# Attention memory of a fused layer: tokens grouped as 4p + j, the decayed sums in 16 narrow matmuls, neighbour pairs on GpSimd

## The reference

```python
write_lines = exterior(w1, w2)          # (B, T, 16, 6), from x of the token before and x
read_lines = exterior(r1, r2)           # (B, T, 16, 6)
outer = Jw[..., :, None] * Jw[..., None, :]            # 6 x 6 for each token and head
M = exclusive cumsum over tokens of outer * decay**-pos, times decay**pos
rd_M = einsum('bhti,bhtij->bhtj', rd, M)
mem_score = (1 - alpha) * sum(rd_M * rd) + alpha * sum(rd_M * rd_M)
gated = mean over heads of sigmoid(mem_score * mem_scale) * gate
out = (softmax attention + gated * mem_val) @ out_w.T + out_b
```

## Time and profile before

| | us |
|---|---|
| median of 3 executions | 1076.8 (1074.87 to 1082.2) |
| the profiled execution, its own time | 1076.55 |
| its span | 1074.9 |
| PE busy | 948.6 (88%) |
| DVE busy | 738.0 (69%) |
| ACT busy | 603.7 (56%) |
| POOL busy | 444.0 (41%) |
| mean granted clock of PE, share of full speed | 0.949 |

### The profile page before, as it was taken

The page is one execution under the profiler, slowest core; times in us unless marked ns, Lnnn a source line. Parts: engine busy times, 40 slices in busy tenths (PEclk is TensorE's granted clock), DMA queues, the critical chain, the costliest instruction groups (busy, mean ns, idle before and its releaser), DMA issues. The chain is left out here.

```text
span 1074.9 us, 26814 instructions
## 1 busy us (share of the span) xinstructions
PE 948.6 (88%) x8038; PEld 686.6 (64%) x8039; DVE 738.0 (69%) x2668; ACT 603.7 (56%) x1358; POOL 444.0 (41%) x398
## 2 busy tenths in 40 slices
PE   3698999897998997989979889999989989999970
PEld 1244656554655564565545668888879869889860
DVE  4637797795896996978868668876555655555663
ACT  3155554562563554545535668776676656666653
POOL 6437064273363543654544633322322433222243
PEclk8689999998999999999999999999999989999995
DMA  4785103213124033032030453232333323323264
GB/s 140 247 216 141 31 22 124 56 57 117 38 71 119 24 95 85 2 125 55 21 129 12 139 188 85 45 51 48 49 46 60 73 49 53 48 49 49 41 204 159
DMA packets 60852, 90.38 MB, mean 84 GB/s; under 512 B 8700, under 2 KB 50192, under 8 KB 59696
## 3 DMA queue, kind: packets, MB, share of 16 engines
q1 hardware_dynamic: 45336, 62.20, 20.4%
q0 software_dynamic: 14112, 22.42, 11.2%
q10 hardware_dynamic: 1280, 4.19, 1.0%
HBM read 52.79 MB, written 35.86 MB: 82 GB/s over the span
## 5 line engine op out<-in xcount | busy, mean ns | idle before, releaser
L1926 DVE CUSTOM_DVE_ANT_0 junk<-sm,mask_ts 128x512 bf16<-128x512 f32 (+3 forms) x512 | 220.4, 487 | 58.0 <-PE sm L1366 55.8
L1110 ACT ACTIVATE arena_b<-st 128x512 f32<-128x512 f32 x320 | 180.9, 599 | 136.7 <-PE st L1328 89.8
L950 POOL DMA_INDIRECT sums<-arena_b x66 | 109.9, 1666 | 273.9 <-DVE arena_b L2135 263.6
L2098 DVE TENSOR_TENSOR arena_b<-arena_b 128x256 f16<-128x256 f32 x280 | 116.4, 427 | 109.6 <-ACT arena_b L1185 99.4
L1326 PE MATMUL st<-arena_a 128*128 128x384 f16 (+3 forms) x512 | 129.4, 309 | 29.0 <-issue 19.0
L1366 PE MATMUL sm<-arena_a 128*128 128x512 f16 (+3 forms) x512 | 113.7, 311 | 12.1 <-DVE maxes L1926 6.2
L1518 PE MATMUL st<-arena_b,arena_a 128*128 128x256 f16 x840 | 116.2, 276 | 1.6 <-ACT arena_b L1185 1.6
L1518 PE MATMUL sm<-arena_b,arena_a 128*128 128x256 f16 x840 | 115.1, 273 | 2.3 <-issue 2.3
L1531 PE MATMUL pv<-arena_a,arena_b 128*128 x864 | 116.7, 273 | 0.0
L1531 PE MATMUL sm<-arena_a,arena_b 128*128 x816 | 112.9, 274 | 3.1 <-issue 3.1
L1326 PEld LDWEIGHTS st<-arena_a 128*128 128x128 f16 x512 | 50.9, 99 | 87.0 <-issue 45.2
(11 more groups left out here) (335 smaller groups left out, 1756.5 us busy)
## 6 DMA issues: line engine op xcount, KB each, us to landing
arena_b<-slots SPq DMA_DIRECT2D x35, 260.0 KB
arena_a<-w SPq DMA_DIRECT2D x8, 1024.0 KB, 6.2
arena_b<-x_tr SPq DMA_DIRECT2D x8, 512.0 KB, 4.1
q_rows<-arena_b SPq DMA_DIRECT2D x32, 128.0 KB
k_rows<-arena_b SPq DMA_DIRECT2D x32, 128.0 KB
arena_a<-q_rows SPq DMA_DIRECT2D x32, 128.0 KB
arena_a<-k_rows SPq DMA_DIRECT2D x32, 128.0 KB
res<-x_tok POOLq DMA_DIRECT2D x8, 512.0 KB, 6.4
```

The lines of the kernel that those rows point to most:

```text
L950: pool.indirect_dma_start(sums, bass.IndirectOffsetOnAxis(ap=token_now[:, 1 - par, m:m + 1], axis=0), y_out[1 - par][:, m, :], None, compu ...
L1110: act.activation(probs[:, q, :], st_ps[piece % 2][:, :], ACT.Exp, scale=SCORE_SCALE).then_inc(exp_done, 1)
L1926: last = dve.tensor_tensor_reduce(junk[:, n % 3, at:at + width], sm_ps[n % 3][:, at:at + width], mask_ts[:, T - width:T], 1.0, NEG, ALU.ad ...
L2098: dve.tensor_tensor(g_lo[par][:, hc, :], g_32[:, hc % 4, :], g_hi[par][:, hc, :], ALU.subtract).then_inc(hid_done, 1)
```

## The change

**Token order.** Outside attention proper, partition p now holds the four tokens 4p + j, j = 0 to 3. The loads and stores of the residual, the token numbers, and the weights that PE loads for `values_in` (second half), `lines_in` and `o_tokens` follow it: they are taken with a step of four elements. `values_in` becomes two matmuls of 256 columns in place of one of 512, since its first half stays in the old order.

**Memory.** GpSimd sums the four scaled outer products of a partition (L943 of the changed kernel) in place of building the two extra blocks; PE has one matmul of 36 columns for each head, in two stages of eight heads. What the four tokens of one partition give to each other, six pairs, is worked out on GpSimd (L914 to L922, and L948 to L959) and added by DVE in `memory_scores`. GpSimd has 28 linked instructions in place of 16, with the first pair work ahead of its wait for the norms and the rest behind the signal `outer_done`. DVE multiplies each of the two banks with four read lines in turn (L2015) and reduces 1152 elements at once.

**Start.** The decay table halves, and GpSimd builds two small tables (`tables_of_powers`: powers of the decay for the six pairs) ahead of step 1. **Order.** The stage table is rewritten: two `memory` stages stand where six stood, `z` 0 and some others move.

```diff
+("gates", 0), ("logits", 0), ("values", 6), ("scores", 29), ("maxima", 14), ("memory", 0), ("maxima", 15), ("scores", 30),
+("scores", 31), ("maxima", 16), ("tables", 0), ("scores", 32), ("values", 7), ("rank", 0), ("first_weights", 3),
+("first_expert", 0), ("maxima", 17), ("maxima", 18), ("scores", 33), ("maxima", 19), ("values", 8), ("memory", 1),
+("scores", 34), ("maxima_rows", 0), ("scores", 35), ("scores", 36), ("scores", 37), ("first_rows", 0), ("scores", 38),
...
-sp.dma_start(sums[bass.ds(value(b * T), T), :].rearrange("(c p) d -> p c d", p=P), res_of[par][:, :, 0:D]).then_inc(x1_out_s, 16)
+sp.dma_start(sums[bass.ds(value(b * T), T), :].rearrange("(p c) d -> p c d", c=C), res_of[par][:, :, 0:D]).then_inc(x1_out_s, 16)
...
+    write, read = (lines[:, k, :, :].rearrange("p (c h) e -> p c h e", c=C) for k in range(2))
+    for own in range(C - 1):
+        m, at = C - 1 - own, FIRST_PAIR[own]
+        seen = chain(pool.tensor_tensor(pair_parts[:, at:at + m], read[:, own + 1:C, :, ::-1],
+                                        write[:, own:own + 1].broadcast_to([P, m, H, NL]), ALU.mult))
+    pool.wait_ge(pool_chain, n_of(seen))
+    seen = chain(pool.tensor_tensor(pair_parts[:, :, :, 0:3], pair_parts[:, :, :, 0:3], pair_parts[:, :, :, 3:6], ALU.add))
+    for e in (1, 2):
+        pool.wait_ge(pool_chain, n_of(seen))
+        seen = chain(pool.tensor_tensor(pair_parts[:, :, :, 0], pair_parts[:, :, :, 0], pair_parts[:, :, :, e], ALU.add))
+    pool.wait_ge(pool_chain, n_of(seen))
+    seen = chain(pool.tensor_tensor(pair_gain, pair_parts[:, :, :, 0], pair_table[:, :, :], ALU.mult))
     pool.wait_ge(ninv_done, n_of(b + 1))
     if not later(i, 2):
         pool.wait_ge(fill_out, 16 * (E + 1))
-    seen = chain(pool.tensor_tensor(t2[:, 0, :, :], lines[:, 0, :, :], ninv[:, 0, :].unsqueeze(2).broadcast_to([P, H * C, NL]), ALU.mult))
+    by_line = lambda v: v.unsqueeze(2).broadcast_to([P, H * C, NL])
+    chain(pool.tensor_tensor(t2[:, 0, :, :], lines[:, 0, :, :], by_line(ninv_later[:, :]), ALU.mult))
+    seen = chain(pool.tensor_tensor(read_scaled, lines[:, 1, :, :], by_line(own_power[:, :, :].rearrange("p c h -> p (c h)")), ALU.mult))
     pool.wait_ge(pool_chain, n_of(seen))
     if later(i, 2):
-        pool.wait_ge(cs_ready, n_of(6 * b))
+        pool.wait_ge(cs_ready, n_of(2 * b))
     else:
         pool.wait_ge(turned, 4)
         pool.wait_ge(c_read, 1)
-    by_line = lambda v: v[:, 0, :, :].rearrange("p (h c) a -> p h c a", c=C)
     for c4 in range(C):
-        seen = chain(pool.tensor_tensor(outer[:, :, c4, :].rearrange("p h (a e) -> p h a e", a=NL),
-                                        by_line(lines)[:, :, c4, :].unsqueeze(3).broadcast_to([P, H, NL, NL]),
-                                        by_line(t2)[:, :, c4, :].unsqueeze(2).broadcast_to([P, H, NL, NL]), ALU.mult))
-    for dst, before_it, own in ((C, C - 1, 0), (C + 1, C, 1)):
-        pool.wait_ge(pool_chain, n_of(seen))
-        seen = chain(pool.tensor_tensor(outer[:, :, dst, :], outer[:, :, before_it, :],
-                                        delta[:, :].unsqueeze(2).broadcast_to([P, H, NL * NL]), ALU.mult))
-        pool.wait_ge(pool_chain, n_of(seen))
-        left = pool.tensor_tensor(outer[:, :, dst, :], outer[:, :, dst, :], outer[:, :, own, :], ALU.add)
-        if dst == C:
-            seen = chain(left)
-    left.then_inc(outer_done, 1)
+        seen = chain(pool.tensor_tensor(outer[:, c4, :, :].rearrange("p h (a e) -> p h a e", a=NL),
+                                        write[:, c4, :, :].unsqueeze(3).broadcast_to([P, H, NL, NL]),
+                                        t2[:, 0, H * c4:H * c4 + H, :].unsqueeze(2).broadcast_to([P, H, NL, NL]), ALU.mult))
+    for to, of in ((0, 1), (2, 3), (0, 2)):
+        if (to, of) != (2, 3):
+            pool.wait_ge(pool_chain, n_of(seen))
+        last = pool.tensor_tensor(outer[:, to, :, :], outer[:, to, :, :], outer[:, of, :, :], ALU.add)
+        if of != 2:
+            seen = chain(last)
+    last.then_inc(outer_done, 1)
+    seen = chain(pool.tensor_tensor(write_unit.rearrange("p c h e -> p (c h) e"), lines[:, 0, 0:3 * H, :],
+                                    ninv[:, 0, 0:3 * H].unsqueeze(2).broadcast_to([P, 3 * H, NL]), ALU.mult))
+    pool.wait_ge(pool_chain, n_of(seen))
+    for own in range(C - 1):
+        m, at = C - 1 - own, FIRST_PAIR[own]
+        to = near_rows[:, 1:C] if own == 0 else pair_parts[:, at:at + m]
+        seen = chain(pool.tensor_tensor(to, pair_gain[:, at:at + m].unsqueeze(3).broadcast_to([P, m, H, NL]),
+                                        write_unit[:, own:own + 1].broadcast_to([P, m, H, NL]), ALU.mult))
+    pool.wait_ge(pool_chain, n_of(seen))
+    seen = chain(pool.tensor_tensor(near_rows[:, 2:C], near_rows[:, 2:C], pair_parts[:, 3:5], ALU.add))
+    pool.wait_ge(pool_chain, n_of(seen))
+    pool.tensor_tensor(near_rows[:, 3:C], near_rows[:, 3:C], pair_parts[:, 5:6], ALU.add).then_inc(near_done, 1)
     assert link[0] == N, link
...
-    project(out[:, :], 1 - par, COL_VM, 512, 2 + n * P, True).then_inc(vm_ready, 1)
+    project(out[:, 0:D], 1 - par, COL_VM, D, slice(2 + n * P, 2 + n * P + P), True)
+    project(out[:, D:2 * D], 1 - par, COL_VM + D, D, slice(2 + n, 2 + T, C), False).then_inc(vm_ready, 1)
 def lines_in(n):
     b = i - 1
     out = bank(1, ln_done, 4 * b + n + 1)
-    project(out[:, 0:64], 1 - par, COL_W1, 64, 1 + n * P, True)
-    last = project(out[:, 64:272], 1 - par, COL_LN, 208, 2 + n * P, False)
+    project(out[:, 0:64], 1 - par, COL_W1, 64, slice(1 + n, 1 + T, C), True)
+    last = project(out[:, 64:272], 1 - par, COL_LN, 208, slice(2 + n, 2 + T, C), False)
...
-    out = bank(q % 2, cs_read, 6 * b + q + 1)
-    size = C * NL * NL
-    for hl, h in enumerate(range(3 * q, min(3 * q + 3, H))):
-        pe.matmul(out[:, hl * size:(hl + 1) * size], decay_t[:, h, 0:P], outer[:, h, 0:C, :].rearrange("p c e -> p (c e)"),
-                  start=hl == 0, stop=False, skip_group_check=True)
-        last = pe.matmul(out[:, hl * size:(hl + 1) * size - NL * NL], decay_t[:, h, P:2 * P],
-                         outer[:, h, C - 1:C + 2, :].rearrange("p c e -> p (c e)"), start=False, stop=True, skip_group_check=True)
+    out = bank(q, cs_read, 2 * b + q + 1)
+    size, heads = NL * NL, H // 2
+    for hl in range(heads):
+        last = pe.matmul(out[:, hl * size:(hl + 1) * size], decay_t[:, heads * q + hl, :], outer[:, 0, heads * q + hl, :],
+                         start=hl == 0, stop=hl == heads - 1, skip_group_check=True)
     last.then_inc(cs_ready, 1)
 def o_to_tokens(n):
...
         pe.wait_ge(o_evac, n_of(4 * b + 4))
     out = bank(n % 2, ot_read, 4 * b + n + 1)
     for g in range(4):
-        last = pe.transpose(out[:, g * P:(g + 1) * P], o_t[:, g, n * P:(n + 1) * P], ident[:, :])
+        last = pe.transpose(out[:, g * P:(g + 1) * P], o_t[:, g, n::C], ident[:, :])
...
-    l0 = 3 * q * C
-    nl = min(3 * C, H * C - l0)
-    dve.wait_ge(cs_ready, n_of(6 * b + q + 1))
+    heads = H // 2
+    dve.wait_ge(cs_ready, n_of(2 * b + q + 1))
     if q:
         m_wait()
-    dve.tensor_tensor(mr[:, 0:nl, :, :], ms_ps[q % 2][:, 0:nl * 36].rearrange("p (l a e) -> p l a e", a=NL, e=NL),
-                      lines[:, 1, l0:l0 + nl, ::-1].unsqueeze(2).broadcast_to([P, nl, NL, NL]), ALU.mult).then_inc(cs_read, 1)
-    dve.wait_ge(cs_read, n_of(6 * b + q + 1))
-    m_chain(dve.tensor_reduce(rdm[:, l0:l0 + nl, :], mr[:, 0:nl, :, :], AX.X, ALU.add))
-NS, NG = 9, 5
+    for n in range(C):
+        rows = read_scaled[:, H * n + heads * q:H * n + heads * q + heads, ::-1]
+        last = dve.tensor_tensor(mr[:, n], ms_ps[q][:, 0:heads * NL * NL].rearrange("p (h a e) -> p h a e", a=NL, e=NL),
+                                 rows.unsqueeze(2).broadcast_to([P, heads, NL, NL]), ALU.mult)
+    last.then_inc(cs_read, 1)
+    dve.wait_ge(cs_read, n_of(2 * b + q + 1))
+    m_chain(dve.tensor_reduce(rdm[:, q].rearrange("p c h a -> p (c h a)"), mr.rearrange("p c h a e -> p (c h a) e"), AX.X, ALU.add))
...
     dve.wait_ge(dve_chain_m, n_of(NM * (b + 1)))
-    s_chain(dve.tensor_tensor(rp, rdm[:, :, :], lines[:, 1, :, ::-1], ALU.mult))
+    dve.wait_ge(near_done, n_of(b + 1))
+    flat = lambda v: v[:, :, :, :, :].rearrange("p q c h e -> p (q c h) e")
+    by_half = lambda v: v.rearrange("p q c h e -> p q c (h e)")
+    s_chain(dve.tensor_tensor(by_half(rdm[:, :, 1:C]), by_half(rdm[:, :, 1:C]), near_rows[:, 1:C].rearrange("p c (q h) e -> p q c (h e)", q=2), ALU.add))
     s_wait()
-    s_chain(dve.tensor_reduce(s12[:, 0, :], rp, AX.X, ALU.add))
+    for q in range(2):
+        s_chain(dve.tensor_tensor(rp[:, q], rdm[:, q], lines[:, 1, :, ::-1].rearrange("p (c q h) e -> p q c h e", c=C, q=2)[:, q], ALU.mult))
```

180 lines of the change are left out of this document (105 added, 75 removed).

## The result

The changed kernel takes 1094.9 us (median of 6 runs, 1088.85 to 1098.15) where the kernel before takes 1080.0 beside it: 1.0135 times as long, 95% interval 1.0093 to 1.0178. The forecast was 1054 us, 0.979. The profiled execution took 1098.15 us, 21.6 more than the one before; between the medians lie 14.9 us, since it was the longest of its six.

A forecast was written before the change was run, and what follows sets the result against it. PE was taken to bound the kernel (65.94 of 72 us busy), DVE second. Per sequence 3.8 - 0.1 - 0.6 - 0.3 = 2.8 us, 22.4 for eight, off 1076.55: 1054 us; 8-in-10 range 1036 to 1075.

The forecast's parts named there:

- Memory on PE: PE's memory passes: 32 fewer at 0.115 us each, a gain of 3.8 us per sequence, 30.4 us for eight.
- Projections and strided loads: PE's split projection matmuls and weight loads with a step of four: 0.1 us per sequence, strided loads taken as free.
- rival 2: PE's strided weight loads cost near their bound and eat the gain: 1074 to 1091 us, chance 0.12.
- VectorE: Products, reductions and additions on DVE sum to +0.3 us; with 14.6 us idle in a step, nothing on the path.
- GpSimd: Pair work and outer sums on POOL: +8 us per sequence, fitting into its waits, none on the path.
- The start: Tables built on POOL where it waits 24.59 us, and as many DMAs as before: no cost.
- The order: Five score pieces now follow one another with little between: 0.6 us per sequence; other moves nothing to half a microsecond.
- The sum: 3.8 - 0.1 - 0.6 - 0.3 = 2.8 us gained per sequence, 22.4 us for eight, giving 1054 us.
- The collisions: DVE's small operations held beside POOL's new work: a cost of 0.3 us per sequence.
- rival 1: DVE and POOL block each other, in `choose` and beside the norms, so DVE ends the step: 1089 us, chance 0.08.
- Rival 3: Late handoffs during the scatter absorb half of the 2.8 us in seven steps: 1064 us, chance 0.14.

The follow-up runs named there:

- h3: The kernel before without the second memory pass of each head (16 fp32 matmuls of 108 columns), nothing else changed: 0.9777 of the kernel before, prompt chip.
- e2: The kernel before with the new order of stages, no other change: 1.0125 times the kernel before, prompt chip.
- f2: The changed kernel with the new order up to the stage maxima 0 and the old order behind it: 0.9955 of the kernel before, prompt chip.
- k1: The changed kernel, old order behind maxima 0, both reads of the memory sums behind the routing and last maxima, additions where they were: 0.995 of the kernel before.
- f0: The changed kernel itself, run again on a prompt chip: 1.0003 times the kernel before.
- e1: The changed kernel with the stages in the order of the kernel before, all else of the change kept: 0.9948 of the kernel before, prompt chip.
- k2: The changed kernel, old order behind maxima 0, late reads of the memory sums, GpSimd's bias additions behind the last z product: 0.9722 of the kernel before.
- g2: The changed kernel with GpSimd's bias additions waiting for the step's last z product, nothing left out: 1.0014 times the kernel before, late chip.
- g1: The kernel before with GpSimd's two bias additions cut to 8 columns each: 0.9921 of the kernel before, late chip.
- g0: The kernel before itself, run again for its trace on a late chip: 1.0006 times the kernel before.
- e4: The kernel before with each step's eight indirect scatter DMAs replaced by plain stores on SyncE's queue: 0.9806 of the kernel before, prompt chip.
- e3: The changed kernel with each step's eight indirect scatter DMAs replaced by plain stores on SyncE's queue: 0.9919 of the kernel before, prompt chip.

## Why the prediction was wrong

**Memory on PE, forecast 3.8 us a sequence: right.** 0.113 us a pass for 0.115, and h3 shows that such a saving, by itself and on a prompt chip, is worth 24 of its 26 us.

**Projections and strided loads, forecast 0.1 us: about 0.3.** By form, PE:

```profile
L1332 PE MATMUL ms<-arena_b 128*128 128x64 f16 x192 | 12.3, 203 | 12.4 <-DVE zs L2071 12.4
L1457 PE MATMUL ms<-ident,o_t 128*128 128x128 f32 x128 | 23.6, 324 | 1.1 <-DVE zs L2071 1.1
```

From start to start (medians) the fp32 transposes of `o_tokens` take 0.122 us where they took 0.109, sixteen of them 0.2 us more. The lines_in matmuls of 64 columns take 0.035 against 0.029, 24 of them 0.1 us more, those of 208 and 256 columns what the rate of before gives. In e2, which has the new order and the old loads, both have the old values. The Trainium skill, "SBUF — State Buffer", "Door 1: The DMA port swizzle", has a step of 16 bytes read at a lower rate; by that rule the trace agrees for fp32, with an eighth, not the doubling that bounded rival 2. What 64 columns show for fp16, 0.006 us with a step of 8 bytes, that rule doesn't give. Rival 2 is out.

**VectorE, forecast +0.3 us and "nothing on the path": this is the step that failed.** By form, after, and the short reductions of before, which rows 7 don't have:

```profile
L2015 DVE TENSOR_TENSOR outer_home<-ms,t 128x288 f32<-128x288 f32 x64 | 24.8, 450 | 4.0 <-PE ms L1447 4.0
L2019 DVE TENSOR_REDUCE rdm<-outer_home 128x192 f32<-128x1152 f32 x16 | 21.6, 1353 | 0.6
```

```profile
L1964 DVE TENSOR_REDUCE rdm<-mr 128x24 f32<-128x144 f32 x8 | 2.4, 303 | 0.3
```

The reads take 46.4 us for 53.3, 0.9 us less a sequence, and `memory_scores` takes 0.6 more: the size came out at -0.3 us. What failed is the place. I set 14.6 us of idle time in a step against it, an average. In the last 30 us before the routing ends VectorE idles 1.96 us before the change:

```profile
369.70:399.70 30.00, 28.64 (x246) 17.91 (x248) 28.04 (x119) 17.21 (x37) 14.56 (x12) 1.00 0.25 77
```

There the matrix work that left (28.64 to 26.68) brought nothing, and B grew by 0.8 us a sequence. Ahead of the routing's end VectorE had two reads of 1.2 us and now has one of 2.9, and `choose` takes 3.6 for 3.1; maxima queue behind them. The runs show that these reads are on the path of B. With the old second half of the order B is 149.5 us over six sequences (f2), and 140.3 when nothing but the reads moves behind the routing (k1). With the saving alone, six small reads and the old order, it is 139.7 (h3). The forecast had them at nothing; they cost 1.5 us a sequence of B in that order, about 1.0 in the new one (145.8, f0).

**GpSimd, forecast +8 us hidden: right by the trace** (504.7 us busy for 444.0, 7.6 a sequence; no run leaves the new work out). Its own timeline:

```profile
388.38 0.86 POOL L927 TENSOR_TENSOR t<-lines,ninv_later 128x384 f32<-128x384 f32 x1 [1.56 <-DVE ninv_later L1995]
...
394.94 4.27 POOL L943 TENSOR_TENSOR outer_home<-outer_home 128x576 f32<-128x576 f32 x3
...
411.09 1.01 POOL L858 DMA_INDIRECT slots<-res,slot_i  x1 [8.49 <-DVE slot_i L1968]
```

The wait for the norms fell from 4.55 to 1.56 and the scatter still waits 8.5. `choose` beside the new work lost about 0.5 us a sequence, for 0.3 forecast. The start, forecast at nothing, shows 1.6 us up to the first routing, less than two traces of one kernel differ there, and the part behind the last one in a step 3.1; neither was followed up.

**The order, forecast −0.6 and "nothing to half a microsecond either way": about as forecast for the changed kernel.** New against old order costs it 0.5% of the time, 0.7 us a sequence (f0, e1), all of it in the second half as far as the runs can tell (f2). It costs the old sums 1.25%, 1.6 us a sequence (e2).

**The sum.** Against 3.8 us saved I set 0.1 + 0.6 + 0.3, 1.0 us a sequence. On a prompt chip the saving alone gives 0.9777 (h3) and the whole change 1.0003 (f0): everything else in it costs 24 us, 3.0 a sequence. Of the 21.3 us between these two traces 6.0 lie in B, where k1 shows the cause, and 7.4 in A, for which no run names one; the rest is start and end. Moving the reads alone (k1) gives no time back until the additions are moved too (k2), so no run puts a price in time on the reads alone. From the end of one routing to the next a step takes 75.3 us after in the mean of the six and 72.5 before, where I had forecast about 69.

**The collisions, forecast −0.3.** I looked for them beside GpSimd's *new* work (rival 1) and not beside work that the change didn't touch. The end of a sequence's routing fixes when the residual is loaded and so when the old additions run; whatever moves VectorE's chain against it can meet them. But they don't explain what the change lost on a prompt chip, since h3, in the old order and with the old reads, is held as long as f0, 16.6 us. On a late chip they cost some 4.5 us more than before, by way of `memory_scores`. Rival 1 named a mechanism that is there, at another place; that its 1089 us lie near the measured 1094.9 is luck, as it is a small part of them. The Trainium skill, "SBUF — State Buffer", "Who interferes with whom", describes the lock on a shared port that lasts a whole instruction; by that rule the trace agrees, 5.88 us for 1.67.

**Rival 3, late handoffs: in part.** In the 12 us above PE works 7.98 before and 6.20 after on a late chip, and o_tokens starts 14.9 us behind the scatter's first DMA for 15.1: it waits as long with less to do. The prediction took the late handoffs for a property of the kernel; in f0, on a prompt chip, o_tokens starts after 7.8 us. With the additions out of the way (g2) the changed kernel is only level with the kernel before, and 0.9% above the kernel before without additions (g1).

**The clock, for which the prediction has no term.** In that stretch PE's granted clock, a mean over both levels, falls from 0.86 to 0.74. Four microseconds each, the changed kernel while PE idles and then when o_tokens begins, and the kernel before at the same place:

```profile
420.00:424.00 4.00, 0.91 (x16) 0.26 (x12) 0.00 (x0) 0.60 (x1) 1.74 (x2) 0.50 0.20 73
424.00:428.00 4.00, 4.00 (x21) 2.41 (x14) 2.15 (x7) 1.19 (x2) 0.04 (x1) 0.50 0.86 222
```

```profile
414.00:418.00 4.00, 3.19 (x25) 2.08 (x22) 2.56 (x8) 2.29 (x4) 0.00 (x0) 1.00 0.90 214
```

In both kernels the clock falls behind 4 us in which PE works some 1.5 (406 to 410 before, 412 to 416 after); before, it is back when o_tokens begins. After, PE then works without a gap at 1.2 GHz where it worked at 2.4: a matmul of 512 columns is busy 0.63 us for 0.38 (timelines of PE). Over the six sequences PE is busy at the lower level for 55.9 us after, 32.5 before (25.9 in g0) and 39.0 in g2. At half the clock at most half of the 23 us more is lost, so up to 12 us by this estimate, more than the additions. What share of the late chip's loss is the clock, and what the stretch itself, no run settles: those with plain stores landed on a prompt chip, and neither the saving alone nor the old order without the wait was run on a late one.

Also open: the kernel before with its additions behind z. e4 (0.9806, z held in one of the six sequences) stands only 0.8% above k2, so much of k2's gain may be had without the change. And A on a prompt chip without collisions is 41.6 and 41.4 us in e4, 42.1 and 41.5 in e3, though the latter has less matrix work; the rows name no single wait for that.
